# Products without a reader on TensorE, in its first idle stretch and ahead of the output projection of a cross-attention and expert kernel

## The reference

```
x = x + xattn(context, layernorm(x))
x = x + ffn(layernorm(x))

xattn: queries from the 1024 tokens, keys and values from context and tokens together (77 + 1024);
       16 heads of 64; q and k are RMS-normalised; out = softmax(q k^T) v;  result = out @ Wout + bout
ffn:   shared = gelu(t @ Wfc_s + bfc_s) @ Wproj_s + bproj_s
       gate   = the two largest of softmax(t @ Wr) over 8 experts, scaled to sum 1
       routed = sum over the two experts of gate * (gelu(t @ Wfc[e] + bfc[e]) @ Wproj[e] + bproj[e])
       result = shared + routed
```

## Time and profile before

| | |
|---|---|
| median of 3 runs | 2645.99 us (2645.78 to 2649.12) |
| the profiled execution, its own time | 2644.76 us |
| its span | 2643.1 us |
| TensorE busy with matmuls | 2502.3 us, 95% |
| VectorE, ScalarE, GpSimd busy | 1857.7, 1691.6, 1312.2 us |
| mean granted clock of TensorE | 0.978 |

### The profile page before, as it was taken

One profiled execution on the slowest core, in us unless ns is written; L12 is line 12 of the kernel. 1 busy time (PEld: TensorE's weight loads), 2 busy tenths in 40 slices (PEclk: granted clock), 3 DMA queues, 4 the chain that ended last, 5 costly groups with the idle time before them and its releaser, 6 DMA issues. The chain is left out here.

```text
span 2643.1 us, 45087 instructions
## 1 busy us (share of the span) xinstructions
PE 2502.3 (95%) x14568; PEld 2048.0 (77%) x14568; DVE 1857.7 (70%) x2507; ACT 1691.6 (64%) x2286; POOL 1312.2 (50%) x784
## 2 busy tenths in 40 slices
PE   3699999999999999999999999986989999999998
PEld 3577777777777777777777777754989999999997
DVE  6666776767777777677677767765877557776775
ACT  2477777777777777778778777774332334454453
POOL 4344553555444544454445544541542526666675
PEclk8799999999999999999999999998989999999999
DMA  5665556545664566455655565545741449999996
GB/s 186 193 159 141 155 156 165 152 134 167 165 157 133 161 162 169 131 169 151 163 148 142 162 166 149 137 131 122 169 122 55 141 145 319 321 321 321 325 320 176
DMA packets 256912, 466.62 MB, mean 177 GB/s; under 512 B 65575, under 2 KB 145755, under 8 KB 251848
## 3 DMA queue, kind: packets, MB, share of 16 engines
q1 hardware_dynamic: 230166, 406.54, 54.6%
q0 software_dynamic: 25696, 58.82, 7.9%
q10 hardware_dynamic: 978, 0.34, 0.1%
HBM read 280.90 MB, written 79.85 MB: 136 GB/s over the span
## 5 line engine op out<-in xcount | busy, mean ns | idle before, releaser
L664 DVE TENSOR_TENSOR pr_lo<-pr,pr_hi 128x1024 fp32r<-128x1024 f32 x576 | 818.5, 1429 | 356.1 <-ACT pr_hi L765 350.6
L764 ACT ACTIVATE pr<-ps_s 128x1024 f32<-128x1024 f32 x512 | 525.9, 1027 | 332.9 <-PE ps_s L883 313.5
L765 ACT ACTIVATE pr_hi<-ps_s 128x1024 fp32r<-128x1024 f32 x512 | 522.1, 1020 | 0.0
L897 PE MATMUL ps_o<-pr_hi,vA 128*65 128x512 f32 x1152 | 464.9, 404 | 20.6 <-DVE o_second L603 11.3
L410 POOL TENSOR_TENSOR sq<-raw 128x1024 f32<-128x1024 f32 (+1 forms) x96 | 183.6, 1913 | 584.6 <-ACT raw L719 584.6
L899 PE MATMUL ps_o<-pr_lo,vA 128*65 128x512 f32 x1152 | 455.1, 395 | 0.0
L898 PE MATMUL ps_o<-pr_hi,vC 128*65 128x512 f32 x1152 | 453.2, 393 | 0.0
L1547 ACT ACTIVATE ht<-f_ps_h,b 128x256 f32<-128x256 f32 x440 | 184.6, 470 | 339.7 <-PE f_ps_h L1479 339.6
L414 POOL TENSOR_TENSOR rs<-ss,minus_half 128x16 f32<-128x16 f32 (+1 forms) x96 | 261.0, 2719 | 246.0 <-DVE ss L649 246.0
L883 PE MATMUL ps_s<-qq_hi,kk 128*128 128x512 f32 x1152 | 362.8, 396 | 8.2 <-ACT pr_hi L765 6.6
L883 PE MATMUL ps_s<-qq_lo,kk 128*128 128x512 f32 x1152 | 361.7, 395 | 0.0
(11 more groups left out here) (195 smaller groups left out, 3857.0 us busy)
## 6 DMA issues: line engine op xcount, KB each, us to landing
w<-w1S_dram SPq DMA_DIRECT2D x160, 512.0 KB, 6.0
lnT_sb<-lnT_dram SPq DMA_DIRECT2D x31, 2304.0 KB, 8.5
w2raw<-in_L_ffn_Wproj SPq DMA_DIRECT2D x78, 512.0 KB, 6.9
qq_hi<-q_hi SPq DMA_DIRECT2D x128, 256.0 KB, 4.8
qq_lo<-q_lo SPq DMA_DIRECT2D x128, 256.0 KB, 5.0
kk<-k_hi SPq DMA_DIRECT2D x64, 288.0 KB, 5.1
kk<-k_lo SPq DMA_DIRECT2D x64, 288.0 KB, 5.4
w1S_dram<-cut POOLq DMA_DIRECT2D x36, 512.0 KB, 4.2
```

The source lines that it names most:

```text
L664: v.tensor_tensor(pr_lo[:, d % RING, :], pr[:, d % 2, :], pr_hi[:, d % RING, :].bitcast(F32), ALU.subtract).then_inc(s_lo, 1)
L764: act.activation(pr[:, d % 2, :], ps_s[:, d % 2, :], ACT.Exp, bias=bias)
L765: act.activation(pr_hi[:, d % RING, :], ps_s[:, d % 2, :], ACT.Exp, bias=bias).then_inc(s_exp, 1)
L897: mm(out, upper, pr_hi[:, r, cols], start=k == 0, stop=False)
```

## The change

Two loops are added on TensorE, and nothing else.

```
+            pe.wait_ge(s_zero, 2)
+            for k in range(26):
+                mm(ps_m[0:P, k % 2, 0:WIDE], ident[:, :], empty[:, 0, :], start=True, stop=True)
             for j in range(PREPS):
                 prep(0, j)
...
+            for k in range(36):
+                nc.tensor.matmul(ps_l[:, 0:256], o_second[DH:P, 0:P], o_second[DH:P, 512:768], start=True, stop=True)
             pe.wait_ge(s_id, 2)
             pe.wait_ge(s_wr, 16)
             batches(pe, batch)
```

## The result

The changed kernel takes 2657.76 us, the median of 6 runs (2655.36 to 2660.91), against 2645.89 (2643.56 to 2650.99, 6 runs) for the kernel before: a ratio of 1.0044, with a 95% interval of 1.0032 to 1.0056. It is slower by 11.9 us; no change was forecast: 2646.0, with 2642.4 to 2650.6 as range. The profiled execution's span is 2653.8 us, 10.7 longer than before.

What follows compares the result with a forecast made beforehand. VectorE and the weights' load, not TensorE, bound the first 39 us; VectorE's chain sets the output projection. 2644.76 + 0 + 0 = 2644.8; the runs' median lies 1.2 higher, giving 2646.0, range 2642.4 to 2650.6.

Steps and rivals of the forecast that it cites:

- The clock is full when they begin, and they keep TensorE busy: 36 x 0.51 = 18.4: Ahead of the output projection: 36 products from 1818.4 end at 1836.8; value 0, ends 0 and +2 us.
- a clock at 0.50 through the added products: Sign named in advance that the forecast is wrong: the added products run at a clock of 0.50.
- the clock falls at 1820.4 all the same and rises again after 4.0 to 6.0 us of work: Second-loop variant: loop ends 2 to 3 us later, 1838.8 to 1839.8, slip 1.1 to 2.1; second-loop-past case has chance 0.14.
- a clock that doesn't rise: Rival at the start: 26 products at 1.02 end at 30.6, first transposes 9.7 us late; 2655.2 us, chance 0.08.
- The slack of 2.8 us: Output projection: 2.8 us between the end of the first group's products (1841.11) and VectorE taking their sums (1843.92).
- The price: Both loops: a plain float32 product takes 0.51 us, ends 0.25 and 0.59, twice that at the low clock.
- My low end of 0.25: Both loops: lowest price of an added product, 0.25 us, two records at twice one fp32r product's full-clock cost.
- The first loop: Start: 26 products from 4.1 us end at 20.4, before the first transpose is ready; value 0, ends 0 and +1.
- the 16 transposes didn't run in half their time: Sign of being right, at the start: transposes at 20.97 in half their time, from 3.99 to about 2.2 us.
- Even both places paid in full stay within it: Start and output projection: returning 1.8 us each, 3.6 together, stays within the 0.2% (5.3 us) indistinguishable from no change.
- the slower rival: Start: clock doesn't rise during the first loop, adding 9.2 us, 2655.2; chance 0.08; range reached about half its loss.
- The stretch from 39.4 begins at the low clock as before: After the start: TensorE idles from 31.5 to 39.4 as before, so its next work begins at the low clock.

Runs made afterwards that it cites:

- with full partitions: Against the kernel before: no first loop; the 36 products ahead of the output projection read a tile of ones over 128 partitions; 2645.87 us, ratio 0.9998.
- the run with one gap: Against the kernel before: neither added loop; 14 products over 128 partitions in front of the third projected tile; 2642.93 us, ratio 0.9987.
- the run with 18 products: Against the kernel before: only the loop ahead of the output projection, with 18 products instead of 36; 2646.39 us, ratio 1.0001.

## Why the prediction was wrong

- **The step that failed** is, in the second loop, "The clock is full when they begin, and they keep TensorE busy: 36 x 0.51 = 18.4". They kept TensorE busy, 1.79 of 1.80 and 27.20 of 27.20 us, and didn't keep its clock: 32 of the 36 ran at a clock of 0.50, 0.85 us each, and the loop took 29.19 us for 18.4 and ended at 1848.3 for 1836.8. This is one of the signs of being wrong that I had named ("a clock at 0.50 through the added products"), and TensorE as what VectorE's addition waits for is another. Even the variant in which "the clock falls at 1820.4 all the same and rises again after 4.0 to 6.0 us of work" took its recovery from stretches of 128 partitions; the products' other shape, 64 partitions, is in the diff and I passed over it. One of my rivals came near, a clock that doesn't rise, but I gave it to the other loop, whose products are full.
- What it cost follows from my own steps with the measured prices: 4 products in 1.8 us and 32 at 0.85, from 1819.1 to 1848.3; then the 48 real products, 16 in 3.4 us and the others in 4.2, end 1855.8; VectorE takes them at 1855.89 for 1843.92 + 0.7. That is 11.3 late for the 11.9 measured. The slack of 2.8 us was read rightly for that execution; it varies with the broadcast (in the changed kernel's it would be 4.2, the multiplication's end at 1846.9 less 1834.9 + 7.8) and is too small in either.
- **The price.** 0.51 us for a plain float32 product was too high: 0.43 at the full clock, 0.85 to 0.87 at 0.50. My low end of 0.25 was far off. With 0.43 and a full clock the second loop would have lasted 15.5 us (an estimate, 36 x 0.43) and fitted; so this error worked against a loss and doesn't explain it.
- **The first loop**: right. The clock rose after 4.5 us (4.0 to 6.0 forecast), the end at 17.9 lay before 20.97 (2.5 earlier than my 20.4, since the price was too high), and the time didn't change (0.9998). One sign failed without harm: the 16 transposes didn't run in half their time, because the clock fell again among them. That VectorE's splits and the weights' load cover TensorE there was shown from the other side, too: 5.9 us of delay passed through to L723 as 5.5, so the slack was about the 0.5 read from the earlier trace rows.
- **"Even both places paid in full stay within it"** (within 0.2%): neither place paid anything that can be seen, at full clock either (0.9998 for each, alone and with full partitions; the intervals leave up to 3 us).
- **The range** ended at half of the slower rival. Nothing in it covered a loop of 36 at the low clock throughout, which by rows 4 and 5 was 36 x 1.02 = 36.7 us, to 1855.1, 15 beyond the latest end that I allowed; the case should have had its own chance beside the first loop's.
- "The stretch from 39.4 begins at the low clock as before" was right, and the run with one gap shows that this stretch, which I priced nowhere, is on the path.

## What to carry to other kernels

Products that only keep the clock up should look like the ones that they stand in for: here those over all 128 partitions raised it (after 4.5 us at the start, within 6 us at the projection) and those over the upper 64 didn't (0.50 for 27 to 31 us). They should end before the work behind them is ready even at the low clock, here at 0.85 to 0.87 us for each; one look at the granted clock during the filler tells. Fill the idle stretch whose *following* products are on the path, found by who waits for TensorE behind it, not the longest one. An order of magnitude: two stretches filled for nothing, one half as long worth 0.13% by the medians and 0.06% by the one pair of profiles.

## What the runs showed of the hardware

- Plain float32 products over the upper 64 partitions left the granted clock at 0.50 for 27 to 31 us of unbroken work at the output projection, with two kinds of data, and by their durations (0.87 us each) for 22.7 us at the start, with a third; the same over 128 partitions raised it in 4.5 us (start) and within 6 us (projection). Busy products alone didn't raise the clock here: in these stretches TensorE's busy share is 1.0 (27.20 of 27.20 us in the changed kernel), and it stays at 0.50.
- The start's transposes didn't hold a full clock in these runs: in the run with only the first loop, with 3.4 idle us ahead of them, it was at 0.71 in the mean of 21 to 22 us and at 0.50 from 22 on (16 in 3.64 us). Yet behind 16 of the same kind, from 92.5 to 96.5, it went from 0.50 to 0.97.
- Whether the clock is 1.00 or 0.50 when the output projection opens differs from run to run: 0.99 in 1818.4 to 1820.4 in the profile of the kernel before, 0.50 from 1818 on (0.67 in the mean of the us before) in the run with 18 products, in which all instructions until then are the same.
